# An end point moved: dequantisation jobs spread up to the second layer's attention, in place of the experts' gate

## The reference

```
x = x + L0_xattn(layernorm(x), ctx)       # 16 heads of 96, keys are context and x itself
x = x + L0_ffn(layernorm(x))              # ternary weights, 512 -> 1376 -> 512, rounded to whole numbers
x = x + L1_xattn(layernorm(x), ctx)       # softmax(x ctx^T) ctx, no weights
x = x + L1_ffn(layernorm(x))              # low-rank experts, top 16 of 64
x = x + L2_xattn(layernorm(x), ctx)
x = x + L2_ffn(layernorm(x))              # gate over three experts, top 2
x = x + L3_xattn(layernorm(x), ctx)
x = x + L3_ffn(layernorm(x), w1, w2, w3)  # the three weights are dequantised first
```

```
absmax = max|block|;  normalized = block / absmax
dq = CODE[searchsorted(bounds, normalized)] * absmax     # CODE has 16 values, so 15 bounds
gate = x dq1^T;  up = x dq2^T;  out = (silu(gate) * up) dq3^T
```

## Time and profile before

| What | Value |
|---|---|
| median of three executions | 1754.61 us (1748.97 to 1754.72) |
| the profiled execution | 1750.64 us, span of its instructions 1748.9 us |
| PE busy | 1451.7 us, 83% |
| DVE busy | 1115.7 us, 64% |
| PE L1991, the code sums | 169.7 us in 495 matmuls |
| DVE L1595, the comparisons | 233.6 us in 495 instructions |
| attention of layer 0 | up to about 633 us |
| feed-forward part of layer 0 | about 633 to 877 us |
| layer 1 and the attention of layer 2 | about 877 to 1139 us |

### The profile page before, as it was taken

The page is one execution under the profiler, slowest core; times in us unless marked ns, Lnnn a source line. Parts: engine busy times, 40 slices in busy tenths (PEclk is TensorE's granted clock), DMA queues, the critical chain, the costliest instruction groups (busy, mean ns, idle before and its releaser), DMA issues.

```text
span 1748.9 us, 19188 instructions
## 1 busy us (share of the span) xinstructions
PE 1451.7 (83%) x6585; PEld 1150.0 (66%) x6585; DVE 1115.7 (64%) x2569; ACT 461.4 (26%) x994; POOL 312.8 (18%) x186
## 2 busy tenths in 40 slices
PE   6559999998999889898377878589997566589998
PEld 5347776685776668686266767487886355477786
DVE  4567777768777658767967556634466788854142
ACT  3214423423334323232212113113213222122010
POOL 4101211211112112111121013116422421012120
PEclk9779999999999999899655897569998788799999
DMA  6421331322223221321011013001111000001011
GB/s 202 139 69 51 89 88 49 93 77 64 77 67 84 64 62 42 84 82 41 24 43 40 23 49 91 17 1 36 46 52 49 25 1 1 1 24 61 13 38 48
DMA packets 99409, 96.42 MB, mean 55 GB/s; under 512 B 13138, under 2 KB 72418, under 8 KB 99314
## 3 DMA queue, kind: packets, MB, share of 16 engines
q1 hardware_dynamic: 98802, 94.35, 18.3%
q0 software_dynamic: 512, 0.85, 0.2%
HBM read 84.34 MB, written 10.82 MB: 54 GB/s over the span
## 4 chain that ended last, share of the span: by engine, by line
PE 62%; DVE 26%; ACT 4%; issue 4%; DMA 2%; SPq 1%; POOL 1%; ACTq 0%; DVEq 0%; POOLq 0%
PE bank L1651 49%; PE bank L1991 5%; PE bank L1743 4%; DVE nf_y L1595 3%; DVE st L1136 2%; DVE xn L1154 1%; PE bank L1676 1%; DVE mx L1504 1%; DVE xT L1113 1%; DVE e L1518 1%; PE bank L1733 1%; DVE sm L1516 1%; DVE mx L1187 1%; PE bank L1947 1%; DMA nf_a<-in_L_w 1%
## 5 line engine op out<-in xcount | busy, mean ns | idle before, releaser
L1651 PE MATMUL bank<-xT,slots 128*128 128x512 f32 (+1 forms) x1920 | 471.2, 404 | 10.4 <-DVE xT L1113 6.9
L1651 PEld LDWEIGHTS bank<-xT,slots 128*128 128x128 f32 (+1 forms) x1920 | 357.1, 187 | 110.9 <-issue 10.2
L808 POOL TENSOR_TENSOR slots<-staging,slots 128x1024 fp32r<-128x1024 f32 (+4 forms) x97 | 230.2, 2376 | 1107.0 <-ACT slots L896 1106.9
L1595 DVE TENSOR_SCALAR nf_y<-nf_w 128x512 fp32r<-128x512 f32 (+2 forms) x495 | 233.6, 499 | 25.7 <-PE bank L1991 24.7
L1651 PE MATMUL bank<-slots,h 128*128 128x512 f32 (+1 forms) x728 | 181.7, 410 | 20.1 <-DVE h L1243 13.9
L1651 PEld LDWEIGHTS bank<-slots,h 128*128 128x128 f32 (+1 forms) x728 | 142.9, 197 | 56.8 <-DVE h L1243 14.8
L1991 PE MATMUL bank<-nf_y,nf_d 128*128 128x512 f32 (+2 forms) x495 | 169.7, 427 | 10.7 <-DVE nf_y L1595 8.5
L896 ACT ACTIVATE slots<-staging 128x1024 fp32r<-128x1024 f32 (+4 forms) x97 | 98.2, 1018 | 189.9 <-PE bank L1651 173.6
L929 ACT ACTIVATE e<-bank,mx 128x320 f32<-128x320 f32 x128 | 66.4, 524 | 272.2 <-DVE mx L1190 268.1
L1209 DVE TENSOR_TENSOR x<-bank,x 128x512 f32<-128x512 f32 x72 | 49.7, 690 | 125.7 <-PE bank L1651 125.6
L1991 PEld LDWEIGHTS bank<-nf_y,nf_d 128*128 128x128 f32 (+1 forms) x495 | 94.9, 197 | 46.9 <-issue 15.6
(11 more groups left out here) (244 smaller groups left out, 1905.0 us busy)
## 6 DMA issues: line engine op xcount, KB each, us to landing
staging<-in_L_wqkT SPq DMA_DIRECT2D x16, 480.0 KB, 3.7
nf_out<-nf_w SPq DMA_DIRECT2D x30, 256.0 KB, 2.1
staging<-nf_out SPq DMA_DIRECT2D x30, 256.0 KB, 2.8
staging<-in_L_woT SPq DMA_DIRECT2D x16, 384.0 KB, 3.3
staging<-in_L_w SPq DMA_DIRECT2D x12, 512.0 KB, 3.9
nf_a<-nf_max SPq DMA_DIRECT2D x40, 128.0 KB, 3.5
nf_r<-nf_rcp SPq DMA_DIRECT2D x40, 128.0 KB, 3.4
nf_w<-in_L_w SPq DMA_DIRECT2D x15, 256.0 KB, 4.2
```

The costliest lines, as they stand in the source:

```text
L808: g.tensor_tensor(lo, split_source(i), hi.bitcast(FP32), ALU.subtract).then_inc(*sig.mark("weight_low", i))
L1595: v.tensor_scalar(nf_y[0:rows, i % STAIR_RING, 0:size], w_, bound, first, compare, ALU.mult)\
L1651: ins = mm(dst, l_, r_, start=i == 0, stop=i == len(passes) - 1)
```

## The change

One constant:

```
-BACKGROUND_END = "gate2"
+BACKGROUND_END = "scores1"
```

## The result

| kernel | median, us | range, runs | profiled execution (span) |
|---|---|---|---|
| before | 1754.66 | 1748.97 to 1759.38, 4 | 1750.64 (1748.9) |
| after | 1793.51 | 1791.59 to 1797.64, 4 | 1797.64 (1795.9) |

The ratio is 1.0226, interval 1.0189 to 1.0263: the change costs about 39 us. The forecast was 1753 us with a range of 1735 to 1775. The result lies outside the range, on the side of the first rival and beyond that rival's 1774.

What follows compares the result with a forecast made beforehand. PE bound layer 0's attention; between 877 and 1139 us PE and DVE waited for each other. Costs 22 + 2.7 + 6 = 30.7 against gains 30 + 2 = 32: -1.3 us, 1753 us, range 1735 to 1775.

Steps and rivals of the forecast that it cites:

- the first rival: Layer 0's attention: each of eight w3 chunks costs PE some 3 us, 24 in all; 1774 us, chance 0.22.
- The gain behind layer 0: Layer 1 and layer 2's attention, 877 to 1139 us: dequantisation taken out saves 30 us, between 19.7 and 34.5.
- The bare price of the moved work: Layer 0: 22 us in its attention, less 2 gained in the first 120 us; 2.7 in the feed-forward part.
- The new wait in the down projection: First half of layer 0's down projection: PE waits for a late w3 chunk, about 6 us, range 0 to 8.
- the chunk of w3: Layer 0's attention: a shorter lead makes each of some eight w3 chunks 1.3 us later.
- the collisions: Layer 0's attention: added comparisons colliding with POOL lose 5.3 us of DVE; 3 us allowed together with late w3 chunks.
- The recorded sign of being wrong: First scores to gate shrinking by less than 20 us, or layer 0 growing by less than 20 or more than 40.
- PE rode through most waits of this kind.: Layer 0's attention: DVE waited 23.0 us for w3 data in six pieces, mostly without holding up PE.
- the ends 15.5 and 59 for the stage: Layer 0's attention cost: lower bound 15.5 us for queue slots, upper 59 with DVE's work and w3 lateness in series.
- The w3 chunks become a bound: Layer 0's attention: denser rhythm makes each w3 chunk cost PE some 3 us, 24 in all; 1774 us, chance 0.22.
- The queue's place is all it costs: Layer 0: PE pays only slots, 15.5 + 2.7 us, and 34.5 comes back behind; 1736 us, chance 0.27.
- The clock falls where the sums leave: Layer 1's experts: with fewer sums the stage falls to the 1.2 GHz level, 27 us lost; 1780 us, chance 0.05.

Runs made afterwards that it cites:

- e10: Changed kernel with ten copies for each w3 chunk in place of twenty, reciprocals first, maxima on their own semaphore: 1749.76 us, ratio 0.9988.
- e11: Changed kernel with ten w3 copies and reciprocals first, but the end point at the end of layer 1's expert products: 1752.91 us, ratio 1.0005.
- e5: Changed kernel with ten copies for each w3 chunk in place of twenty, values unchanged: 1753.08 us, ratio 1.002.
- e3: Changed kernel with four copies for each w3 chunk, which alters w3's values: 1752.4 us, ratio 1.0006.
- e6: Changed kernel with its twenty w3 copies, reciprocals ahead of the maxima, which get their own semaphore: 1753.87 us, ratio 1.0026.
- e7: Kernel before with thirty-two copies for each w3 chunk in place of sixteen to twenty: 1759.4 us, ratio 1.0064.
- e8: Changed kernel with useless matmuls (24, 14 and 24) ahead of the first sum of three chunks: 1784.9 us, ratio 1.0207.

## Why the prediction was wrong, point by point

**What held.** The gain behind layer 0: 30 forecast, 30.0 measured. The balance without w3's copies, which was the idea of the forecast: e10 and e11 say no change. The bare price of the moved work: 22 less 2 for layer 0's attention with the stretch ahead of it, and its end moved from 603.5 to 627.6 us in e5, by 24.1; forecast 2.7 plus 6 for the feed-forward part, and in e5 it grew from 273.4 (603.5 to 876.9) to 281.6 us (627.6 to 909.2), by 8.2. Layer 1's first scores were forecast at 906 and stand at 909.2 there. The new wait in the down projection is where it was put:

```profile
810.24 0.69 DVE L1589 TENSOR_TENSOR nf_w<-nf_w,nf_r 128x512 f32<-128x512 f32 x1 [10.07 <-DMA nf_r<-nf_rcp]
812.48 3.33 PE L1991 MATMUL bank<-nf_y,nf_d 128*128 128x512 f32 x7 [6.19 <-DVE nf_w L1605]
```

Forecast "about 6 us", measured 6.19. A part of that is luck: PE came to the sum 1.4 us later than forecast (19.6 us behind the first product's start, not 18.2), and the sum started later too, because it waited for the ending of the chunk before, which the forecast did not have. And the wait was priced by its length alone. The window grew by 11.1 us, its clock fell to 0.86 from 0.92, and ten copies in place of twenty took 6.7 of it away (37.7 us).

**What failed.** The term "the chunk of w3", 1.3 us for each of eight, together with the collisions put at 3 us. In the changed kernel it was 36.0 us of the stage (551.1 against 515.1 with ten copies; single executions, and that of the changed kernel is its slowest). The recorded sign of being wrong came about with it: layer 0 grew by 80.4 us (its end at 957.3, from 876.9), where more than 40 was to be the sign. DVE's waits for the copies grew by 21.0 us (16.2 to 37.2), twice the 10.4 of eight chunks at 1.3, and PE's waits for the ending by 17.0 (2.1 to 19.1). Three things in the term were wrong:

- "PE rode through most waits of this kind." That was read from PE's short waits in the old rhythm and carried over to the new one. The code said otherwise: the ending of the chunk before stands behind the scaling in DVE's queue, and every first sum needs it. I had followed a late chunk of w3 in the down projection, though without the ending, and not at all in the attention, which has eight of them.
- The clock was weighed only as a loss where the sums leave, not where pauses arise. The stage stood at 0.98 before, with little left to gain and much to lose: 22.1 of the 36.0 us are busy time of equal work.
- The range held the ends 15.5 and 59 for the stage and stopped at 30 for the reason that PE idles little. Idle time of before doesn't bound the idle time of after. The sum's own upper end, 59 for 22, would have given 1790, three us from the result, but by luck: it had no term for the clock, and it put the moved work's time on DVE in series with PE, which e5 doesn't bear out.

The Trainium skill, TensorE: Matmul & The Clock Gate, section HAM oscillation, names idle gaps between bursts as what throttles it again. The prediction cited it for layer 1; it applied to layer 0, and the rows at 349 to 359 us agree.

**The rivals.** "The w3 chunks become a bound" named the place and the mechanism; its 3 us for each chunk left the clock out. "The queue's place is all it costs" is refuted by e3, e5, e6 and e10: even with the copies in time there is no gain. "The clock falls where the sums leave" did not come about as a loss. Layer 1's expert products, the first to the last:

```profile
1029.80:1094.00 64.20, 51.93 (x232) 42.70 (x231) 34.07 (x108) 10.04 (x22) 2.35 (x1) 0.83 0.03 9
```

They took 75.3 us at a clock of 0.86 before (957.3 to 1032.6 us), and take 64.2 at 0.83; the "over 0.85" of the forecast was a little too high.

**What stays open.** Why about the same lateness costs 10 us in the old rhythm and some 39 in the new one. DVE waited about as long in e7 as in the changed kernel, and PE half as long. DVE has a fifth more comparisons to do in the new rhythm, and so less free time to catch up, but no run here varied the rhythm alone at a fixed lateness of DVE. Open too is why the clock fell so often in the changed kernel. Only three of its eleven stretches at the half level, 23.8 of 88 us, are behind the long waits for the ending. Some of the pauses ahead of the others are there with ten copies as well, followed by less of the half level or by none. With the lateness away, 57 of the 88 us are gone (e5), but how it brings the half level behind the short pauses was not followed, and a part of it may be chance, as the two rows of e8 show.

## What to carry to other kernels

When a change makes a background job denser, follow its slowest piece from the first issue to the first waiter on the busiest engine, at each place where it occurs, and count the issues of its DMAs one by one. On an engine that runs at the full clock level, price each new pause by its length and, as a chance, again by a slower stretch behind it (here about 2 us a place where it came). Fix the lateness before judging the placement: with ten DMAs in place of twenty, or the needed half first, the placement itself turned out to be worth nothing that can be told.

## What the runs showed of the hardware

- SP took 0.58 to 0.69 us for each of w3's copies, in series: twenty took 11.7 us or more, ten 6.3. In e7, with copies to 32 partitions each, it was 0.46 to 0.52. DVE began some 1.5 us behind the last issue, so most of the way from the first issue to the first use (14.7 us) was issuing.
- A pause of 6.06 us was followed by about 10 us at the half level, with twelve-pass products at 5.05 us against 2.95. Filling it with useless matmuls of about equal length was worth 2.5 us beside the pause itself, and 2.6 and 1.7 us at two other places.
- Not every shorter pause did that: one of 2.52 us at 354.62 us in e5 left the clock up, one of 2.49 us at 554.38 us in the changed kernel was followed by the half level, and the same pause of 2.49 us at 547.74 us in e8 was not.
- Over the stage, e5 against the changed kernel, 57 us less at the half level gave 22 us back: a microsecond there cost some 0.4 us and not 0.5. That PE's pauses and short matmuls lose less at the half level would explain it, and is not shown.
